# Edges' sums join the rotation of PSUM banks in the last stream of a graph and expert network

## The reference

```python
x = x + L0_gnn(layernorm(x), ...)       # messages t1[src] + (feat[src]*feat[dst]) @ W2, summed over dst
x = x + L0_ffn(layernorm(x), ...)       # feed-forward for the top half of the rows by a router's weight
x = x + L1_gnn(layernorm(x), ...)       # attention over edges, then out + gelu(out @ w1) @ w2
x = x + L1_ffn(layernorm(x), ...)       # eight experts, weighted by a softmax
```

```python
msg = h[src] * alpha[:, :, None]                       # 8 heads of 32
agg = segment_sum(msg, dst, num_segments=N)            # the edges' sums
out = agg.reshape(N, 256) + xn @ W_res + bias
out = layer_norm(out, ln2_g, ln2_b)
ff = gelu_tanh(out @ ffn_w1 + ffn_b1) @ ffn_w2 + ffn_b2
```

## Time and profile before

| | us |
|---|---|
| median of three runs | 2847.34 (2845.98 to 2850.08) |
| span of the profiled execution | 3261.7 |
| PE busy | 2445.7 (75%) |
| DVE busy | 1927.4 (59%) |
| POOL busy | 1783.5 (55%) |
| ACT busy | 1330.1 (41%) |

### The profile page before, as it was taken

How to read it: one execution, slowest core, us unless ns; L and a number is a source line. 1 busy time by engine, 2 the same in 40 slices (tenths; PEclk the granted TensorE clock), 3 DMA queues, 4 the chain that set the end, 5 groups by cost and what they waited for, 6 DMA issues and landing times.

```text
span 3261.7 us, 50094 instructions
## 1 busy us (share of the span) xinstructions
PE 2445.7 (75%) x16869; PEld 1988.4 (61%) x16869; DVE 1927.4 (59%) x5122; ACT 1330.1 (41%) x2771; POOL 1783.5 (55%) x1695
## 2 busy tenths in 40 slices
PE   8437677567676768661567888899888898898998
PEld 8325455345554547660356766777677676686887
DVE  8733344344344447764466676677776676686754
ACT  6303233222222324440234454555544555464665
POOL 6366666666666660837665574465744556464000
PEclk9667777778877778785688998999998999898999
DMA  9443334334443331276467675576765767576534
GB/s 324 142 129 113 118 117 122 110 109 118 119 121 118 113 100 28 88 227 184 138 208 235 191 233 158 181 233 206 224 204 161 219 198 219 177 219 193 160 119 140
DMA packets 312865, 531.11 MB, mean 163 GB/s; under 512 B 89679, under 2 KB 210322, under 8 KB 312598
## 3 DMA queue, kind: packets, MB, share of 16 engines
q1 hardware_dynamic: 234021, 312.19, 30.5%
q0 software_dynamic: 75264, 212.04, 22.8%
q10 hardware_dynamic: 3312, 3.55, 0.4%
HBM read 454.05 MB, written 73.54 MB: 162 GB/s over the span
## 4 chain that ended last, share of the span: by engine, by line
PE 30%; another core or an unknown queue 9%; DVE 6%; issue 5%; ACT 2%; POOL 1%; DMA 1%; SPq 1%; DVEq 0%; POOLq 0%; ACTq 0%
PE PB L125 25%; PE PB L2793 2%; POOL G L2766 1%; DVE G L3092 1%; ACT TFm L3006 1%; DVE XR L3273 1%; DVE H2l L3261 1%; PE PB L2804 0%; DVE H1l L3261 0%; DMA G<-tab,SRCL 0%; PE PB L2845 0%; DVE HT9l L3182 0%; PE PB L2814 0%; PE PB L2880 0%
## 5 line engine op out<-in xcount | busy, mean ns | idle before, releaser
L2766 POOL DMA_INDIRECT G<-tab,SRCL x784 | 905.8, 1155 | 694.8 <-PE PB L2793 442.8
L1194 POOL DMA_INDIRECT GE<-tab,SRCL x748 | 724.0, 968 | 393.9 <-issue 204.1
L3006 ACT ACTIVATE TFm<-PB,BIA,SCL 128x512 f32<-128x512 f32 (+2 forms) x416 | 312.8, 754 | 474.4 <-PE PB L125 226.0
L125 PE MATMUL PB<-YTMh,MW 128*128 128x512 f32 (+2 forms) x832 | 303.8, 416 | 51.6 <-ACT TFm L3006 36.4
L125 PE MATMUL PB<-H1h,MW 128*128 128x512 f32 (+2 forms) x832 | 299.8, 412 | 37.9 <-issue 29.0
L125 PE MATMUL PB<-MW,H2h 128*128 128x256 f32 x1568 | 301.4, 291 | 27.3 <-issue 20.3
L125 PEld LDWEIGHTS PB<-MW,H2h 128*128 128x128 f32 x1568 | 253.9, 197 | 36.1 <-issue 24.9
L3092 DVE TENSOR_TENSOR G<-G 128x1024 f32<-128x1024 f32 x196 | 238.1, 1216 | 2.7 <-DVE G L3086 2.2
L125 PE MATMUL PB<-MW,H2l 128*128 128x256 f32 x784 | 224.7, 287 | 4.7 <-issue 4.7
L1578 ACT ACTIVATE TF<-PB,fb 128x256 f32<-128x256 f32 (+1 forms) x200 | 93.6, 472 | 323.1 <-remote 165.9
L125 PEld LDWEIGHTS PB<-YTMh,MW 128*128 128x128 f32 x832 | 167.7, 204 | 93.9 <-issue 42.8
(11 more groups left out here) (365 smaller groups left out, 6614.6 us busy)
## 6 DMA issues: line engine op xcount, KB each, us to landing
MW<-msplit SPq DMA_DIRECT2D x312, 512.0 KB
ROW<-relrow SPq DMA_DIRECT2D x196, 96.0 KB
msplit<-FWs SPq DMA_DIRECT2D x68, 256.0 KB
part<-ZERO SPq DMA_DIRECT2D x2, 6600.0 KB
G<-tab,SRCL POOLq DMA_INDIRECT x784
GE<-tab,SRCL POOLq DMA_INDIRECT x748
part<-WIN SPq DMA_DIRECT2D x262, 33.0 KB
SUMa<-part SPq DMA_DIRECT2D x49, 132.0 KB
```

The source lines that it names most:

```text
L125: ins = pe.matmul(ps, lhs(p), rhs(q), start=(first and i == 0), stop=(last and i == 2), skip_group_check=True)
L1194: po.indirect_dma_start(c.GE[:, (s - 2 * UE) % RU, q, 0:256], None, c.tab0, bass.IndirectOffsetOnAxis(ap=c.SRCL[:, 2 * s + q:2 * s + q + 1 ...
L2766: po.indirect_dma_start(b.G[:, j % RP, u, :], None, c.tab1, bass.IndirectOffsetOnAxis(ap=c.SRCL[:, 4 * j + u:4 * j + u + 1].bitcast(U32), ...
L3006: a.activation(b.TM[:, m, 0:n], PB[of][:, 0:n], ACT.Relu, bias=b.BIA[:, l, q:q + 1], scale=b.SCL[:, l, q:q + 1]).then_inc(S.h2_relu if l e ...
```

## The change

The four banks 2, 3, 4 and 6 go round, and `sums` is one of the steps that take them in turn. The planner gets the same: `sums` asks for a bank in turn and frees it with `evac`, and no longer names the evacuation of the window before as a need. In `last_pe` the wait for that evacuation is replaced by the wait that every rotating step has, ahead of the first unit; `last_act` reads the bank that the table gives.

```diff
-ROUND = (3, 4, 6)
+ROUND = (2, 3, 4, 6)
-ROTATING = ("turn_rows", "hidden", "layer", "xturn", "router", "share_turn", "bo")
+ROTATING = ("sums", "turn_rows", "hidden", "layer", "xturn", "router", "share_turn", "bo")
@@ work_of
             add("PE", ("sums", w), 0.3 + 0.44 * (j - 3 * w + 1), [
-                *((name, i) for name in ("onehot", "weigh") for i in range(3 * w, j + 1)), w and ("evac", w - 1)], lag=DRAIN)
+                *((name, i) for name in ("onehot", "weigh") for i in range(3 * w, j + 1))], lag=DRAIN, bank="turn", frees=("evac", w))
@@ last_pe
         if step == "sums":
             w, = x
+            to = bank_of[step, w]
+            bank(to)
             for j in range(3 * w, last_unit(w) + 1):
                 on.wait_ge(S.onehot, j + 1)
                 on.wait_ge(S.product, j + 1)
-                if j == 3 * w and w:
-                    on.wait_ge(S.evac, w)
                 for u in range(4):
-                    ins = pe.matmul(PB[2][Q * u:Q * u + Q, 0:264], b.OR2[:, j % RL, u, :], b.G[:, j % RP, u, 0:264],
+                    ins = pe.matmul(PB[to][Q * u:Q * u + Q, 0:264], b.OR2[:, j % RL, u, :], b.G[:, j % RP, u, 0:264],
                                     start=(j == 3 * w), stop=(j == last_unit(w)))
                 ins.then_inc(S.edge_mm, 1)
+            free[to] = (S.evac, w + 1)
@@ last_act
-            a.copy(b.WIN[:, w % RV, :], PB[2][:, 0:264]).then_inc(S.evac, 1)
+            a.copy(b.WIN[:, w % RV, :], PB[bank_of["sums", w]][:, 0:264]).then_inc(S.evac, 1)
```

## The result

The changed kernel takes 2860.93 us (2855.04 to 2871.44, 14 runs) against 2850.91 us (2844.67 to 2858.0, 14 runs) for the kernel before: ratio 1.0037, 95% interval 1.0026 to 1.0048. It is slower by 10 us, where I had forecast 27 us faster.

A forecast was written before the change was run, and what follows sets the result against it. PE's program, run in written order, was taken as the bound. Gains of 25 (banks) and 10 (clock) less 5 (sums) gave 30 us of the profiled execution, taken as 27 of 2847.3: 2820 us, range 2788 to 2866.

The forecast's parts named there:

- 221 us of idle time: PE's idle time in the mixed stretch from 1600 to 3065 us of the profile, taken as what matters.
- (1): PE's waits for rotating banks after 1600 us: 85.7 us in 40 gaps, of which a fourth bank gains 25 us.
- signs of being wrong: Prediction wrong if ACT's stalls are of the profile alone, or the order changes more than the banks do.
- factor of nine tenths: Cut the 30 us gain of the profiled execution to 27 us, should ACT's stalls be shorter outside the profile.
- slack of the next six steps: Per bank gap, the smaller of gap and least data slack in six following PE steps was counted: 25.2 us.
- (2): PE's clock in the last stream: fewer falls behind bank gaps, nothing to 60 us gained, taken as 10 us.
- (3): Sums joining PE's rotation: new waits for the bank's old reader and ACT's copy cost 0 to 15 us, priced 5.
- Rival B: Late copies of sums on ACT hold up PE's rotation: 28 us cost against 13 gain, about 2862 us; chance 0.10.
- (4): Planner's new orders on PE, ACT, DVE and SP: up to 25 us either way, taken as nothing.
- Rival C: The new order is worse: nodes or sums later, experts' tail after 3065 us grows, about 2862 us; chance 0.13.
- 436 us of POOL's waiting: POOL's waits for PE to finish edges' sums in the mixed stretch, taken as slack hiding a worse gather order.
- The rule of rotation: Skill's advice to rotate independent products through PSUM banks and use all eight; alone it makes a gain, no figure.

The follow-up runs named there:

- e1: Four banks in rotation with the sums among them, every engine's order as in the kernel before: 2848.14 us, ratio 1.0001 to the kernel before.
- e18: Four banks in rotation, sums among them, in exactly the order of the kernel before, timed in the 3265 us condition: 3271.1 us, ratio 1.0023.
- e17: The changed kernel itself once more, in the 3265 us condition: 3288.38 us against 3258.4 for the kernel before, ratio 1.0113.
- e6: Exactly the orders of e3, but with the sums in rotation over four banks: 2812.61 us, ratio 0.9866 to the kernel before.
- e3: The kernel before with planner constant HOP at 0.07 for 0.06, which moves 681 of PE's 1380 steps; banks unchanged: 2811.14 us, ratio 0.9875.
- e14: The changed kernel planned with constant SPARE at 0.12 for 0.10, in the 3265 us condition: 3351.34 us, ratio 1.026 to the kernel before.
- e16: The changed kernel planned with a sum's unit cost at 0.43 for 0.44, in the 3265 us condition: 3324.86 us, ratio 1.0138 to the kernel before.
- e2: The changed kernel's orders on every engine, but the kernel before's three rotating banks and bank 2 for sums: 2857.25 us, ratio 1.0033.

## Why the prediction was wrong, step by step

**What bounds the kernel.** PE's program as the bound was right, more so than I wrote (97% busy where the earlier trace rows have 85%). The error was to take 221 us of idle time as the kernel's. I noted that the profiled execution was 414 us longer than the median and guessed that most of these lay in the gather-paced stretch. The stream from its first `factors` to its last layer takes 1775 us in that trace and 1521 in the other: 254 of the 414 lie in the very stream on which the sum rests, not in the gather-paced stretch. PE's work in it, which I wrote can't shrink much, is 1459 us in the one and 1369 in the other for the same 10042 matmul records; the other 164 us are idle time.

**(1) Bank waits, 25 us: the step that failed.** In the measured condition they are 1 us, and e1 gives 1.0001. My text named as signs of being wrong that the stalls of ACT are of the profile alone, and that the order changes more than the banks do; the first holds for the condition that was timed, and the second holds. The factor of nine tenths by which I took the gain over to the median was the place to act on it. In the other condition the waits are real and do vanish, but e18 gains nothing (the interval ends at 0.9991, 3 us). My slack of the next six steps counted each gap by itself. What it left out is most likely that ACT's and DVE's later steps stand behind the same stall, so that PE meets it again further on: the longer waits at `output`, `factors` and `turn_rows` fit this, but no run isolates it.

**(2) The clock, 10 us.** 0.98 in the mixed stretch before and after; 0.90 in the other condition with four banks (e17, e18), 0.91 with three. Nothing was gained. By the Trainium skill ("TensorE: Matmul & The Clock Gate", A second HAM failure mode: psum-queue depth-cycling), as the prediction read it, more rotation would bring no clock back. The outcome agrees on the size, but no run shows the clock to fall through rotation (e1 has 1.00 in each of its three stretches).

**(3) The sums in the rotation, 5 us lost.** Nothing measurable: e1 1.0001, e6 0.9866 beside e3's 0.9875. Rival B, a late copy that holds the rotation, does not appear: in no trace of a kernel with four banks (after, e1, e6, e14, e16, e17, e18) does a step wait for the copy of a sum.

**(4) The plan, nothing with 25 us either way.** The bound held, the value didn't: e2 gives 9 us lost, the whole result. This is the second step that failed, and the one that turned the sign: a term put at nothing because the trace of before can't show it. Rival C had the right cause and the wrong picture: the tail behind the last sum is unchanged (196 and 195 us), the loss is in three stretches of the mixed part, and the last sum ends 17 us later in the trace, not 20 to 40 earlier. That I priced the one edit that touches 382 of PE's steps at zero, and the edit of the banks, which touches none, at 30 us, was the wrong way round. The 436 us of POOL's waiting that were to hide a worse order in the gathers were 95 us in the measured condition, with DVE already waiting 48 us for gathered rows.

**The rule of rotation.** The Trainium skill asks to rotate independent products through different PSUM banks and to use all eight ("Perfetto Trace Analysis", Optimizing Tensor Performance and Matmul Optimizations), and that alone would have made this a gain. Here it is not borne out: a fourth bank with the old lists gives 1.0001 and 1.0023. In the first case the rotation was waited for 1 us in all, so there was nothing to gain; in the second the waits moved.

The measured time lies in the range I gave only because the range took in rivals B and C as well; no part of my sum leads there. The chance of "slower" was 0.23, for two mechanisms, and the cause of one of them, C, came true at another place than I named.

## What to carry to other kernels

Set the span of a profile against the measured median before anything else: if they differ by 15%, as here, its idle times belong to a condition and not to the kernel, and gains read from them have to be worked out again from a profile of the condition that is timed. When a planner writes the order, any edit of its inputs is a new order: run the edit with the old order and the new order with the old code, two kernels that split the effect at once, and draw some neighbours of the plan (0.07 for 0.06 gave 1.25%) before judging the edit. A wait that is removed behind a stalled engine can come back at the next thing that the engine owes, as here at the low halves.

## What the runs showed of the hardware

The same program takes 2850 or 3265 us, in two conditions that last over whole series of executions; chip number 7 of the record has series of both. In the longer one ACT and DVE stand, from 1600 us on, for up to 16 and 10 us before instructions whose releaser the trace can't name (ACT before relus 190.1 us in 52 waits, 203.1 in 59 in e18). It is not a matter of the last stream: in the trace of before such waits of ACT sum to 728 us, in 177 waits, from 200 us on. In the traces of before and of the change in the other condition no wait has that name. The packets of the DMA queues take the same mean time in both traces of before (68 ns in the large queue, 158 and 157 ns in that of the gathers). ACT's gaps over 4 us after 1600 us do not fall together with the loading of instructions more often than by chance (17 of 41, where 20 are expected). What stalls the engines stays open.
